# Eleven of 24 gate-times-up tiles on GpSimd as 32-bit integers, the others' up factors in PSUM, and the sigmoid's rounding held behind the product in front

## What is computed

```python
x = act_qdq(x)
up = act_qdq(x @ lpbq_dequant(w_up).T)
gate = act_qdq(x @ lpbq_dequant(w_gate).T)
sig = fixed_qdq_u16(jax.nn.sigmoid(gate))
gate = act_qdq(gate * sig)
o = act_qdq(gate * up)
return o @ lpbq_dequant(w_down).T
```

## Time and profile before

| | us |
|---|---|
| median of three runs | 843.31 (842.41 to 846.26) |
| the profiled execution | 843.56 |
| its span | 841.8 |
| PE busy | 686.2 |
| DVE busy | 666.8 |
| ACT busy | 494.0 |
| POOL busy | 250.1 |

### The profile page before, as it was taken

The page is one execution under the profiler, slowest core; times in us unless marked ns, Lnnn a source line. Parts: engine busy times, 40 slices in busy tenths (PEclk is TensorE's granted clock), DMA queues, the critical chain, the costliest instruction groups (busy, mean ns, idle before and its releaser), DMA issues.

```text
span 841.8 us, 11634 instructions
## 1 busy us (share of the span) xinstructions
PE 686.2 (82%) x4087; PEld 523.3 (62%) x4087; DVE 666.8 (79%) x1308; ACT 494.0 (59%) x625; POOL 250.1 (30%) x201
## 2 busy tenths in 40 slices
PE   6971058999999778999999999999999991007998
PEld 5660036988888534656656665578878771006998
DVE  5988884878786479997887867978887888996654
ACT  2222013434543336886887868656649886995873
POOL 4444412566777512220222020015314433100000
PEclk9995559999999959999999999999999996558999
DMA  9926713466533730020031000032206441101342
GB/s 299 345 84 233 246 14 121 116 176 166 142 61 45 213 120 1 1 71 2 1 121 51 26 27 1 25 126 101 101 1 209 141 149 50 50 0 51 101 150 100
DMA packets 59539, 84.93 MB, mean 101 GB/s; under 512 B 7905, under 2 KB 47713, under 8 KB 57953
## 3 DMA queue, kind: packets, MB, share of 16 engines
q1 hardware_dynamic: 50224, 61.35, 21.8%
q0 software_dynamic: 7872, 21.11, 10.3%
q10 hardware_dynamic: 1392, 1.82, 0.6%
HBM read 53.73 MB, written 30.54 MB: 100 GB/s over the span
## 4 chain that ended last, share of the span: by engine, by line
PE 56%; DVE 22%; ACT 8%; issue 3%; POOL 1%; DMA 1%; SPq 0%; DVEq 0%; ACTq 0%; POOLq 0%
PE bank L2257 10%; PE bank L1998 8%; PE bank L2051 7%; PE bank L2279 5%; DVE peak L1754 4%; PE bank L1407 4%; PE bank L1441 3%; PE bank L1501 3%; PE bank L1464 3%; PE bank L1461 3%; DVE above L777 2%; PE bank L1422 2%; DVE qx L1161 2%; ACT wgateT L1921 1%; PE bank L1445 1%
## 5 line engine op out<-in xcount | busy, mean ns | idle before, releaser
L1286 ACT ACTIVATE x<-bank,bic 128x512 f32<-128x512 f32 x160 | 105.6, 691 | 38.3 <-PE bank L1441 35.8
L1161 DVE TENSOR_REDUCE qx<-bank 128x4 fp32r<-128x616 f32 x128 | 98.2, 796 | 22.8 <-PE bank L1407 21.1
L1998 PE MATMUL bank<-ux,uwh 128*128 128x512 f32 x384 | 98.3, 395 | 1.6 <-ACT low L1895 1.2
L1998 PEld LDWEIGHTS bank<-ux,uwh 128*128 128x128 f32 x384 | 71.9, 189 | 19.7 <-ACT low L1895 2.4
L1441 PE MATMUL bank<-qT,K 128*128 128x512 f32 x128 | 63.3, 505 | 4.2 <-ACT x L1286 1.7
L1407 PE MATMUL bank<-Kb,qTb 128*128 128x308 bf16 x256 | 56.4, 314 | 7.3 <-DVE qx L1161 3.7
L1091 POOL CAST qx<-q 128x1024 fp32r<-128x1024 f32 x8 | 8.5, 1063 | 170.7 <-PE bank L1422 161.2
L2218 ACT ACTIVATE wgateT<-bank 128x512 f32<-128x512 f32 x32 | 19.2, 598 | 66.2 <-PE bank L2257 62.2
L2005 PE MATMUL bank<-uwh 128*128 128x512 f32 x39 | 11.3, 447 | 50.6 <-DVE peak L1754 50.6
L1998 PE MATMUL bank<-ux,uwl 128*128 128x512 f32 x192 | 52.2, 394 | 0.0
L1407 PEld LDWEIGHTS bank<-Kb,qTb 128*128 128x128 bf16 x256 | 18.7, 100 | 51.0 <-DVE qx L1161 23.5
(11 more groups left out here) (392 smaller groups left out, 2010.3 us busy)
## 6 DMA issues: line engine op xcount, KB each, us to landing
xs_dram<-ux POOLq DMA_DIRECT2D x6, 1024.0 KB, 4.4
ux<-xs_dram POOLq DMA_DIRECT2D x6, 1024.0 KB, 5.8
x_dram<-x SPq DMA_DIRECT2D x4, 1024.0 KB, 5.4
xr<-in_w1T SPq DMA_DIRECT2D x8, 512.0 KB
xr<-in_w3T SPq DMA_DIRECT2D x8, 512.0 KB
xr<-in_w2T SPq DMA_DIRECT2D x8, 512.0 KB
row_dram<-xn SPq DMA_DIRECT2D x8, 512.0 KB, 3.0
x_dram<-xr SPq DMA_DIRECT2D x8, 512.0 KB, 2.9
```

The source lines that it names most:

```text
L1161: dve.tensor_reduce(qx[:, k, g * GH:(g + 1) * GH, MROW].rearrange("p (u h) -> p u h", u=2), pair[i][:].rearrange("p (u x) -> p u x", u=2)[ ...
L1286: act.activation(pr[g % 2][h], S_[u % 2], ACT.Exp, bias=bic[:, s // 2, h // GH:h // GH + 1]).then_inc(p_done, 1)
L1998: mm = pe.matmul(bank[j][:, m * TB:(m + 1) * TB], w[:, c * HI + cols:c * HI + cols + P], x[:, part, c * TB:(c + 1) * TB], start=(w is uwh ...
```

## The change

In the up stage POOL's rounding of tile n waits for the product of tile n-1 in place of n-2, and DVE issues its own gate rounding of tile n+2 ahead of the product of tile n.

In the second product the tiles at the odd places 3 to 23 of the order (`POOL_AT`, eleven) are multiplied by POOL, both factors and the result being 32-bit integers in the place of the f32 gate tile. Their gates are rounded in place by ACT (by POOL for place 3), their up factors in place by POOL, for the places 7, 13 and 19 by ACT (`UP_BY_ACT`). The other 13 (`DVE_AT`) stay with DVE, which now reads the up factor from PSUM (`uint`, banks 0 to 2 as int32). All 24 largest values stay with DVE. POOL's three weight subtractions come behind its first, fourth and seventh product. The 28 warming matmuls write bank 3. SP waits for both counters of products.

```diff
+            POOL_AT = tuple(range(3, FT, 2))
+            DVE_AT = tuple(i for i in range(FT) if i not in POOL_AT)
+            UP_BY_ACT = POOL_AT[2::3]
+            uint = [bank[i][:].bitcast(I32) for i in range(3)]
...
-                sp.wait_ge(k_p2, FT)
+                sp.wait_ge(k_p2, len(DVE_AT))
+                sp.wait_ge(k_pg, len(POOL_AT))
...
-                    if n >= 2:
-                        pool.wait_ge(k_p, n - 1)
+                    if n >= 1:
+                        pool.wait_ge(k_p, n)
                     pool.tensor_scalar(sq[n % 3], gslot[n], 65536.0, 1.0, ALU.mult, ALU.mult).then_inc(k_sq, 1)
...
-                pool.wait_ge(m_w, 1)
-                for j in range(PAIRS):
-                    cols = slice(j * TB, (j + 1) * TB)
-                    pool.wait_ge(k_p2, j + 1)
-                    pool.tensor_tensor(uwl[:, cols], wdownT[:].rearrange("p c d -> p (c d)")[:, cols], uwh[:, cols].bitcast(F32),
-                                       ALU.subtract).then_inc(m_w, 1)
+                pool.wait_ge(y_qs, 3)
+                own = FT
+                for k, i in enumerate(POOL_AT):
+                    n = ORDER[i]
+                    whole, upper = pslot[n].bitcast(I32), uslot[UPAT[n]].bitcast(I32)
+                    if k == 0:
+                        pool.tensor_scalar(whole, pslot[n], qs[:, 11:12], 1.0, ALU.mult, ALU.mult).then_inc(k_sq, 1)
+                        own += 1
+                    if i not in UP_BY_ACT:
+                        pool.tensor_scalar(upper, uslot[UPAT[n]], qs[:, 10:11], 1.0, ALU.mult, ALU.mult).then_inc(k_sq, 1)
+                        own += 1
+                    else:
+                        pool.wait_ge(k_uq, ups_done(i))
+                    if k:
+                        pool.wait_ge(k_gq, gates_done(i))
+                    pool.wait_ge(k_sq, own)
+                    pool.tensor_tensor(whole, whole, upper, ALU.mult).then_inc(k_pg, 1)
+                    if k % 3 == 0 and k // 3 < PAIRS:
+                        cols = slice(k // 3 * TB, (k // 3 + 1) * TB)
+                        pool.wait_ge(m_w, 1)
+                        pool.tensor_tensor(uwl[:, cols], wdownT[:].rearrange("p c d -> p (c d)")[:, cols], uwh[:, cols].bitcast(F32),
+                                           ALU.subtract).then_inc(m_w, 1)
...
+                    gate_integers(n + 2)
                     minus_product(n)
-                    gate_integers(n + 2)
...
                 for i in range(FT):
...
+                    elif i in DVE_AT:
+                        dve.wait_ge(k_uq, ups_done(i))
+                    if i in DVE_AT:
+                        dve.wait_ge(k_gq, gates_done(i))
+                        dve.tensor_tensor(pslot[ORDER[i]], gq[DVE_AT.index(i) % 3], uint[DVE_AT.index(i) % 3], ALU.mult).then_inc(k_p2, 1)
                     if i:
                         largest_out(i - 1)
...
-                    act.activation(gq[i % 3], pslot[n], ACT.Copy, scale=qs[:, 11:12]).then_inc(k_gq, 1)
-                    if i:
-                        act.activation(uq[i % 3], uslot[UPAT[n]], ACT.Copy, scale=qs[:, 10:11]).then_inc(k_uq, 1)
+                    if i in DVE_AT:
+                        d = DVE_AT.index(i)
+                        if d >= 3:
+                            act.wait_ge(k_p2, d - 2)
+                        act.activation(gq[d % 3], pslot[n], ACT.Copy, scale=qs[:, 11:12]).then_inc(k_gq, 1)
+                        if d:
+                            act.activation(uint[d % 3], uslot[UPAT[n]], ACT.Copy, scale=qs[:, 10:11]).then_inc(k_uq, 1)
+                    else:
+                        if i != POOL_AT[0]:
+                            act.activation(pslot[n].bitcast(I32), pslot[n], ACT.Copy, scale=qs[:, 11:12]).then_inc(k_gq, 1)
+                        if i in UP_BY_ACT:
+                            act.activation(uslot[UPAT[n]].bitcast(I32), uslot[UPAT[n]], ACT.Copy, scale=qs[:, 10:11]).then_inc(k_uq, 1)
```

More of the change, by code:

```diff
@@ L1628, in build @@
             u_sent, u_back = ([sem(f"u_{n}{i}") for i in range(2)] for n in ("sent", "back"))
-            k_gq, k_gd, k_sg, k_sq, k_p, k_top, k_uq, k_du, k_p2, k_om = (sem("k_" + n) for n in "gq gd sg sq p top uq du p2 om".split())
+            k_gq, k_gd, k_sg, k_sq, k_p, k_top, k_uq, k_du, k_p2, k_pg, k_om = (sem("k_" + n) for n in "gq gd sg sq p top uq du p2 pg om".split())
             k_away, k_home = ([sem(f"k_{n}{i}") for i in range(2)] for n in ("away", "home"))
@@ L1656, in ffn_sync @@
                 for n in (4, 5):
-                    sp.wait_ge(k_uq, ORDER.index(UP[0] * PAIRS + n - 4))
+                    i = ORDER.index(UP[0] * PAIRS + n - 4)
+                    if i in POOL_AT:
+                        sp.wait_ge(k_pg, POOL_AT.index(i) + 1)
+                    else:
+                        sp.wait_ge(k_p2, DVE_AT.index(i) + 1)
                     home(n)
@@ L1679, in ffn_sync, with gates_done, outs, ups_done @@
                 sp.wait_ge(m_out[1], 16 * (NS // 2 + 1))
+            def gates_done(i):
+                return FT - len(GATES_BY_DVE) + sum(k != POOL_AT[0] for k in range(i + 1))
+            def outs(i):
+                return pslot[ORDER[i]].bitcast(I32) if i in POOL_AT else pslot[ORDER[i]]
+            def ups_done(i):
+                return sum(k in DVE_AT[1:] or k in UP_BY_ACT for k in range(i + 1))
             def ffn_gpsimd(pool):
@@ L1828, in largest_out @@
                 def largest_out(i):
-                    dve.wait_ge(k_p2, i + 1)
-                    largest(PK_O + i, pslot[ORDER[i]], k_om)
-                dve.tensor_scalar(uq[0], uslot[UPAT[ORDER[0]]], qs[:, 10:11], None, ALU.mult).then_inc(k_du, 1)
+                    if i in POOL_AT:
+                        dve.wait_ge(k_pg, POOL_AT.index(i) + 1)
+                    else:
+                        dve.wait_ge(k_p2, DVE_AT.index(i) + 1)
+                    largest(PK_O + i, outs(i), k_om)
+                dve.tensor_scalar(uint[0], uslot[UPAT[ORDER[0]]], qs[:, 10:11], None, ALU.mult).then_inc(k_du, 1)
                 for i in range(FT):
@@ L1947, in ffn_scalar @@
                     n = ORDER[i]
-                    if i >= 3:
-                        act.wait_ge(k_p2, i - 2)
                     if n < SPILL:
                         act.wait_ge(k_home[n % 2], 16 * (n // 2) + 16)
-                    act.activation(gq[i % 3], pslot[n], ACT.Copy, scale=qs[:, 11:12]).then_inc(k_gq, 1)
-                    if i:
-                        act.activation(uq[i % 3], uslot[UPAT[n]], ACT.Copy, scale=qs[:, 10:11]).then_inc(k_uq, 1)
+                    if i in DVE_AT:
[5 more added lines that the diff above has]
+                            act.activation(uint[d % 3], uslot[UPAT[n]], ACT.Copy, scale=qs[:, 10:11]).then_inc(k_uq, 1)
+                    else:
+                        if i != POOL_AT[0]:
+                            act.activation(pslot[n].bitcast(I32), pslot[n], ACT.Copy, scale=qs[:, 11:12]).then_inc(k_gq, 1)
+                        if i in UP_BY_ACT:
+                            act.activation(uslot[UPAT[n]].bitcast(I32), uslot[UPAT[n]], ACT.Copy, scale=qs[:, 10:11]).then_inc(k_uq, 1)
                 def out_integers(t):
@@ L1958, in out_integers @@
                         act.wait_ge(m_l, t - 5)
-                    act.activation(oi[t % 6], pslot[ORDER[t]], ACT.Copy, scale=qs[:, 3:4]).then_inc(m_i, 1)
+                    act.activation(oi[t % 6], outs(t), ACT.Copy, scale=qs[:, 3:4]).then_inc(m_i, 1)
                 def first_half(m):
@@ L2001, in product, with kept_warm @@
                     return mm
-                def kept_warm(n):
+                def kept_warm(n, at=2):
                     for _ in range(n):
-                        pe.matmul(bank[2][:, 0:TB], uwh[:, 0:P], uwh[:, 0:TB], start=True, stop=True)
+                        pe.matmul(bank[at][:, 0:TB], uwh[:, 0:P], uwh[:, 0:TB], start=True, stop=True)
                 UPPER, LOWER = ((uwh, 0), (uwl, 0)), ((uwh, 1),)
@@ L2038, in ffn_tensor @@
                 pe.wait_ge(k_om, FT - 4)
-                kept_warm(28)
+                kept_warm(28, 3)
                 spread(3, 1)
```

## The result

| | before | changed |
|---|---|---|
| median, us | 844.72 (842.41 to 846.26, four runs) | 833.24 (831.87 to 834.29, four runs) |
| the profiled execution | 843.56 | 833.49 |
| its span | 841.8 | 831.7 |

The ratio is 0.9865, 95% interval 0.9834 to 0.9897: 11.4 us off by the ratio, with 10.9 forecast. The time, 833.24, lies 0.8 above the 832.4 that was forecast and inside the range of 829.5 to 841. (The kernel before had one more run here, which puts its median at 844.72.)

A forecast was written before the change was run, and what follows sets the result against it. VectorE (DVE), busy 57.1 of 57.9 us, was taken to bound the second product. Gains of 9.4 there and 1.5 in the up stage, 10.9 off 843.56, gave 832.7 profiled, 832.4 median; range 829.5 to 841.

The forecast's parts named there:

- The price of the integer product: Second product: one 1024-column 32-bit integer product on POOL costs 2.43 us, like an f32 two-input pass.
- The dear product: Rival, second product: POOL multiplies integers by a longer route, up to 4.8 us, giving 855.0; chance above 4.1 us 0.13.
- the cases between: Second product: POOL product at 2.7 to 3.35 us, 834 to 839, chance 0.08; at 3.35 to 4.1 us, chance 0.06.
- The collision: Second product: DVE's product beside POOL costs nothing extra with one PSUM operand; rival that it still collides, 841.1, chance 0.07.
- POOL's chain: Second product: POOL's roundings, products, subtractions and idle sum to 43.4 us; its last product ends 45.9 us after the scales.
- the term of 11 x 0.31 = 3.4: Second product: each of POOL's eleven products idles 0.31 us behind POOL's own rounding, 3.4 us in all.
- The warming: Before the last spread: 28 matmuls take 8.11 us and end last, by 1.1 us; spread starts 48.45 us after the scales.
- The up stage: Stretch ahead of the second product: the new wait removes POOL's collision with DVE's product; gain 1.5 us in all.
- Forecast cycle 12.1 and wait 1.2: Up stage: four-tile cycle falls from 12.36 to 12.1 us, ACT's wait from 1.35 to about 1.2; some 1.1 us gained.
- tail from product 20: End of the up stage: from product 20's start to the end 8.9 us instead of 9.5, about 0.5 less.

The follow-up runs named there:

- the run with SBUF: Changed kernel with DVE's up factors back in three int16 SBUF buffers instead of PSUM; 839.43 us, ratio 0.9945.
- The wait alone: Kernel before plus only POOL's sigmoid rounding waiting for the product in front, DVE's gate rounding staying behind the product; 838.74 us, ratio 0.9940.
- the order alone: Kernel before plus only DVE's gate rounding moved ahead of the product, old wait on POOL; 845.30 us, ratio 1.0017.
- the fastest version: Changed kernel with DVE's gate rounding behind the product, 18 warming matmuls, and ACT's up factors at places 13, 19, 23; 824.13 us, ratio 0.9768.
- the front half alone: Kernel before plus both up-stage edits, POOL's new wait and DVE's gate rounding ahead of the product; 842.46 us, ratio 0.9971.
- the warming started earlier: Changed kernel with all 28 warming matmuls started when 18 largest values are there instead of 20; 830.38 us, ratio 0.9827.
- the run with the gate rounding behind: Changed kernel with DVE's gate rounding put back behind the product, POOL's new wait kept; 827.90 us, ratio 0.9814.

## Why the prediction was right

- *The price of the integer product.* Taken as 2.43 from the f32 rows, measured 2.35 to 2.39. The dear product, the rival on the side of slower, is out, and so are the cases between.
- *The collision.* Taken as nothing with one PSUM operand; right, and shown by the run with SBUF: 55.3 us where the sum of POOL's work and DVE's products had given 57.1.
- *POOL's chain.* Forecast to end 45.9 us after the scales, measured 753.53 - 709.80 = 43.7. The step that failed is the term of 11 x 0.31 = 3.4: a POOL compute instruction that waits for the one just in front starts 0.08 to 0.15 us behind it, and only seven of the eleven do so, about 1.0 in all; the others wait for ACT or follow a product. The 0.31 was the row of a DMA behind a product, and does not carry over. Of the 2.4 us less, longer waits for ACT (3.2 in place of 2.4) and roundings of 1.10 in place of 1.05 took back 1.3. The rest is the products: two in a row start 2.31 us apart (730.85 and 733.16), not 2.43, some 1.3 for eleven.
- *The warming.* Forecast to end last, by 1.1 us; measured by 2.9. It started 38.95 us after the scales (forecast 40.3), and took 9.13 us to the spread (forecast 8.11). The duration was taken over from one execution, and across the runs here, where 28 matmuls end last, it varied between 8.0 and 9.3 us. The two errors, 1.4 early and 1.0 long, cancelled nearly: 48.08 for 48.45. So the number of this term was right in part by luck; its mechanism, that the warming and not the tiles ends the stretch, was right.
- *The up stage.* Forecast cycle 12.1 and wait 1.2, measured 12.15 and 1.14; tail from product 20 forecast 8.9 us, measured 707.03 - 697.93 = 9.1; together 1.5 forecast, 1.2 measured. The term was right, but I costed the two edits together, and did not draw from my own layout that they work against each other. The wait alone is worth 5.0 us, the order alone costs 1.5, and together they give 1.2.

## What to carry to other kernels

When a change is a bundle, cost each edit by itself too: here moving one line gave back three quarters of what its neighbour brought. An engine kept warm for a later stage is a term of the critical path as soon as the work beside it gets shorter; look whether the stage behind is fed fast enough to use the warmth at all. And when work moves to GpSimd, look at how many SBUF operands VectorE's concurrent instructions have: one operand in PSUM, in place of SBUF, was worth 7.2 of 9.8 us.

## What the runs showed of the hardware that I had not expected

The matmuls of the down product are spaced in one of two ways at the same granted clock. Two runs with the same code in this stage, the fastest version and the same with 8 warming matmuls, by stretch:

```profile
775.00:795.00 20.00, 20.00 (x179) 20.00 (x178) 11.55 (x11) 15.11 (x15) 0.00 (x0) 1.00 0.35 116
```

```profile
775.00:795.00 20.00, 20.00 (x172) 20.00 (x171) 11.00 (x10) 14.91 (x16) 0.00 (x0) 1.00 0.40 132
```

179 against 172 matmuls in 20 us, 4% apart, both at a granted clock of 1.00; the stage takes 73.7 or 76.5 us. Profiled executions of the front half alone and of the warming started earlier were of the second kind (76.2). Earlier in the kernel there is no such difference: from 580 to 600 us all thirteen traces have 90 matmuls, of 512 columns each. I have not found what sets it. The group does not follow the edits: the front half alone is in the slow one and each of its two edits in the other. But each version was traced once, so it isn't shown that one and the same kernel falls into both. If it does, that would account for part of the spread of a kernel's times (839.2 to 846.0 for the front half, whose profiled execution is the 846.0).

The time until TensorE's clock rises at the start of the warming was not the same either: 28 matmuls that nothing else interrupts took 8.12 us in the run with the gate rounding behind and 9.49 in that with the wait alone. In both, the granted clock is 0.50 in the first 2 us; between 4 and 6 us after the start it is 1.00 in the one and still 0.50 in the other.
